# Feed-forward layers: the first two parts of eight heads' weighted sums in one step, the third alone two steps later

## The reference, cut to what matters

```python
x = x + _L0_ffn_ref(_layernorm(x), W_gate, W_qkv)

gating = softmax(x @ W_gate.T); indicator = one_hot(argmax(gating))
q, k, v = split(x @ W_qkv.T, 3)
k_shared = einsum('bth,bthd->btd', indicator, k)
v_shared = einsum('bth,bthd->btd', indicator * max(gating), v)
att = einsum('bhqd,bkd->bhqk', q, k_shared) / sqrt(hd)
att = softmax(where(causal, att, -inf))
y = einsum('bhqk,bkd->bhqd', att, v_shared)
```

## Time and profile before

| | us |
|---|---|
| median of 3 runs | 946.26 |
| lowest, highest | 945.5, 947.89 |
| the profiled execution | 946.92 |
| its span, first to last instruction | 945.2 |
| PE busy | 875.6 (93%) |
| DVE busy | 706.9 (75%) |
| ACT busy | 528.6 (56%) |
| POOL busy | 436.7 (46%) |
| line 1749 (parts 0 and 1), mean of one PE record | 0.38 |

### The profile page before, as it was taken

How to read it: one execution, slowest core, us unless ns; L and a number is a source line. 1 busy time by engine, 2 the same in 40 slices (tenths; PEclk the granted TensorE clock), 3 DMA queues, 4 the chain that set the end, 5 groups by cost and what they waited for, 6 DMA issues and landing times.

```text
span 945.2 us, 19702 instructions
## 1 busy us (share of the span) xinstructions
PE 875.6 (93%) x6510; PEld 684.5 (72%) x6510; DVE 706.9 (75%) x2331; ACT 528.6 (56%) x1378; POOL 436.7 (46%) x682
## 2 busy tenths in 40 slices
PE   5779999889999999987999999999999998999996
PEld 4667777767776777765888788887888776777763
DVE  6678888888778787664868778686868676888873
ACT  6535555454344555436676766757576761555555
POOL 2458888886766556353202121121202022556655
PEclk9789999999999999989999999999999999999999
DMA  6433333223112564102202020202011021132321
GB/s 200 64 55 57 51 51 56 47 44 47 33 32 54 124 125 126 41 14 45 45 2 45 1 45 2 45 1 46 11 35 37 11 34 35 36 65 48 75 48 35
DMA packets 51284, 46.59 MB, mean 49 GB/s; under 512 B 6624, under 2 KB 48624, under 8 KB 51184
## 3 DMA queue, kind: packets, MB, share of 16 engines
q1 hardware_dynamic: 51184, 45.34, 23.8%
HBM read 11.40 MB, written 2.10 MB: 14 GB/s over the span
## 4 chain that ended last, share of the span: by engine, by line
PE 42%; DVE 6%; issue 3%; ACT 2%; POOL 0%; DMA 0%; POOLq 0%; SPq 0%; ACTq 0%; DVEq 0%
PE bank L286 13%; PE bank L1939 6%; PE bank L1889 5%; PE bank L1947 4%; PE bank L1877 4%; PE bank L1711 3%; PE bank L1723 2%; PE bank L1708 2%; DVE weights L1452 1%; PE bank L1749 1%; ACT weights L984 1%; DVE weights L1442 1%; PE bank L1752 1%; DVE arena L1289 1%; PE bank L332 1%
## 5 line engine op out<-in xcount | busy, mean ns | idle before, releaser
L1289 DVE TENSOR_REDUCE arena<-bank 128x2 f32<-128x512 f32 (+1 forms) x192 | 130.6, 683 | 44.7 <-PE bank L1711 44.1
L905 ACT ACTIVATE weights<-bank 128x512 f32<-128x512 f32 x144 | 85.8, 597 | 112.8 <-PE bank L1723 111.8
L984 ACT ACTIVATE weights<-weights,neg_max 128x128 f32<-128x128 f32 (+1 forms) x256 | 113.7, 449 | 32.3 <-DVE neg_max L1442 32.1
L713 POOL TENSOR_SCALAR_AFFINE_SELECT weights<-weights 128x256 f32<-128x256 f32 x144 | 68.0, 473 | 105.9 <-ACT weights L905 105.8
L1711 PE MATMUL bank<-kf_stack,q_stack 96*128 96x128 f32 (+1 forms) x512 | 110.1, 318 | 0.0
L1442 DVE CUSTOM_DVE_ANT_0 weights<-bank,arena 128x128 f32<-128x128 f32 (+1 forms) x256 | 80.6, 352 | 38.3 <-PE bank L1939 36.3
L1939 PE MATMUL bank<-kbT,arena 128*128 128x128 f32 (+1 forms) x512 | 105.1, 328 | 1.0 <-DVE y L421 0.9
L649 POOL TENSOR_SCALAR weights<-weights 128x512 f32<-128x512 f32 x64 | 97.8, 1539 | 12.1 <-ACT weights L808 12.0
L991 ACT ACTIVATE weights<-bank 128x384 f32<-128x384 f32 x128 | 62.7, 490 | 71.2 <-PE bank L1947 70.4
L1452 DVE TENSOR_SCALAR weights<-weights,inv_sum 128x128 f32<-128x128 f32 (+1 forms) x256 | 84.4, 372 | 4.5
L286 PE MATMUL bank<-x_hi,wb_hi 128*128 128x256 f32 x256 | 83.5, 326 | 2.8 <-DVE q_lo L1432 2.8
(11 more groups left out here) (232 smaller groups left out, 2424.9 us busy)
## 6 DMA issues: line engine op xcount, KB each, us to landing
q_stack<-q_hi SPq DMA_DIRECT2D x96, 128.0 KB, 3.8
arena<-arena SPq DMA_DIRECT2D x64, 128.0 KB, 2.5
q_stack<-q_lo SPq DMA_DIRECT2D x48, 128.0 KB, 4.0
ka_stack<-k_hi SPq DMA_DIRECT2D x32, 76.5 KB, 3.8
x_all<-x SPq DMA_DIRECT2D x8, 256.0 KB, 5.4
st_wo<-b_wo SPq DMA_DIRECT2D x8, 256.0 KB, 3.4
arena<-b_wqn SPq DMA_DIRECT2D x8, 256.0 KB, 3.1
out<-x_all SPq DMA_DIRECT2D x8, 256.0 KB, 2.1
```

Of the source, the lines that this page charges most:

```text
L905: a.activation(s["pT"][(STEPS * b + k) % N_PT], p2[k % 2][:, :], ACT.Exp).then_inc(s["exp"], 1)
L984: last = a.activation(p, p, ACT.Exp, scale=-1.0, bias=neg_max[:, h % 4, t:t + 1], accum_out=sums[:, h % 4, t:t + 1])
L1289: v.tensor_reduce(into, p1[k % 2][:, :].rearrange("p (h k) -> p h k", h=n), AX.X, ALU.max, negate=True).then_inc(s["maxed"], 1)
```

## The change

`attend_f` takes a flag in place of the part's number: without it parts 0 and 1 are issued in one go, with it part 2. Octet 1's first parts move from steps 11 and 1 to step 1, its third stays at step 3. Octet 0's move from steps 5 and 7 to step 7, its third stays at step 9. The matmuls are the same in number and form, and their waits (`oT`, `v_sel`, `causal`) move with part 0.

```diff
-                def attend_f(b, o, part):
+                def attend_f(b, o, second):
...
-                    if part == 0:
+                    if not second:
...
-                    pe.wait_ge(*at(s, "causal", b, 6 * o + (6 if part == 2 else 4)))
-                    for j in range(G):
+                    pe.wait_ge(*at(s, "causal", b, 6 * o + (6 if second else 4)))
+                    for part, j in itertools.product((2,) if second else (0, 1), range(G)):
...
-                    if part == 2:
+                    if second:
                         last.then_inc(s["o_ps"], 1)
...
                     if k in (1, 3) and there(b - 2):
-                        attend_f(b - 2, 1, (k + 1) // 2)
-                    if k in (5, 7, 9, 11) and there(b - 1):
-                        attend_f(b - 1, k // 11, (k - 5) // 2 % 3)
+                        attend_f(b - 2, 1, k == 3)
+                    if k in (7, 9) and there(b - 1):
+                        attend_f(b - 1, 0, k == 9)
```

## The result

| | before | after |
|---|---|---|
| median (14 runs each) | 947.01 us | 949.10 us |
| lowest, highest | 944.7, 948.11 | 946.41, 952.25 |
| after / before | | 1.0025, interval 1.0016 to 1.0034 |
| the profiled execution, its span | 946.92, 945.2 | 948.95, 947.2 |
| mean granted clock of the profiled execution | 0.974 | 0.971 |

The change costs 2.1 us where I forecast 1.3 us of gain; 949.1 lies outside the range. PE is busy 3.6 us less and the kernel is still slower. Three executions that took 997 us or more (two of `keep_oct0`, one of the kernel before) are left out of all medians and ratios.

The account below looks back on a forecast made before the run. PE bounds the kernel in the large, but key copies and the DVE decide at the merges; +1.2 + 0.4 - 0.5 - 0.3 - 1.5 - 0.6 = -1.3 us from 946.26 gives 945.0 us, range 942.7 to 948.5.

Parts of the forecast that it names:

- Octet 1, step 11 to step 1: Batch transitions: step 0 gains 0.32 us, step 1 pays 0.43, so 0.11 lost at each of eleven, sum +1.2.
- Start-up 0.05: Step 0 of a batch: PE starts 0.05 us after ACT has written the stacked keys.
- The rival of the late start-up: Step 0: PE starts 0.37 us or more after the keys, each transition loses 0.43; 948.5 to 949.0, chance 0.08 (start-up over 0.3).
- Octet 0, step 5 to step 7: Interior batches: the DVE decides, so PE's 0.33 us buys nothing; only the gate copies gain 0.09 a batch, sum -0.5.
- The copies: Two DVE gate copies after step 5's projection: 0.24 us in place of 0.33, 0.09 off the DVE's chain.
- Batch 6: Both layers, no normalization any more: the gate copy waits 0.98 us for PE, so the earlier projection gives -0.76 twice.
- Other queues ... that it slows the DVE by some hundredths: POOL's masking comes up to 0.76 us sooner beside DVE work; an effect of hundredths a batch, possible in both directions.
- the -0.3: Batch 1 of FFN1: the gate copy waits 0.18 us more for PE, so with the 0.09 octet 0's merge gains 0.3 once.
- The gain of step 0 is lost whole: +0.4: Batch 2 of FFN0: step 0's projection waits 1.07 us for the DVE (x_lo) anyway, so the merge costs +0.4.
- The ends, taken as 0: Four merges from batch 7 to 8 and in batch 8: each from -0.22 to +0.43 us, taken as 0.

Follow-up runs that it names:

- keep_oct0: The changed kernel with octet 0 of the first batch of FFN0 again in steps 5 and 7: 949.12 us, ratio 1.0021 to the kernel before.
- oct1_only: The kernel before with only octet 1 merged at step 1, octet 0 left at steps 5, 7 and 9: 944.66 us, ratio 0.9986.
- the shifted kernels: The kernel before with four or eight dummy matmuls in step 0 of batch 3, FFN0, delaying all later work: 948.89 and 948.59 us.

## Why the prediction was wrong

- **Octet 1, step 11 to step 1: right.** Start-up 0.05, gain 0.30 for 0.32, loss 0.43, together +0.13 a transition for +0.11 (+0.12 by the batch of oct1_only). The rival of the late start-up, which gives 948.5 to 949.0, hits the number by accident: the batch grew by 0.09 and not by 0.34.
- **Octet 0, step 5 to step 7: right, but for 0.05 a batch.** The copies gave their 0.09; line 1316 beside POOL took 0.05 back. The interior of both layers came to +0.55 where I had +0.5 (to +0.8 against the second profile of before, whose FFN0 is 0.25 shorter). Batch 6 gave -0.77 and -0.78 for -0.76.
- **"Other queues ... that it slows the DVE by some hundredths": the first step that failed.** I saw that POOL's work moves up and gave it hundredths in both directions, without laying POOL's timeline beside the DVE's at each batch. In batch 1 of FFN0 a foreign POOL operation of 1.09 us starts just behind the DVE's small operations; moved up, it costs 0.75. I had read only the chain of an interior batch, where POOL has nothing but masks. In FFN1's batch 1 the -0.3 was lost in the same way, and a -0.40 of the clock ahead of it hid that.
- **"The gain of step 0 is lost whole: +0.4" (batch 2 of FFN0): the second.** The term was right (0.37). What was missing is that idle time has a price of its own: taking work out of a stretch in which PE waits anyway leaves it emptier, and behind two such stretches the clock fell to half for 3 us: +1.5. The prediction took the clock as 1.00 and had no term for it.
- **The ends, taken as 0.** They came out at +0.2 and +0.3 off in the profiled pair, but the shifted kernels show that this is no property of the merges: it is where the falls of the clock land.
- **Sum.** Predicted -1.3; with +0.75 for the collision and +1.5 for the clock that makes +0.95, and with the 0.5 by which the ends came out off, +1.45. The profiles give 690.03 - 688.60 = +1.43 from the first turn on. The remaining 0.6 of the profiled pair lies in the first attention, ahead of the change, where two profiles of the kernel before differ by 1.3 among themselves. That the sum closes to 0.02 is partly luck, since the -0.3 of FFN1's batch 1 stands in it and came from the clock. The forecast of 945.0 also started from 946.26, the median of three runs, where fourteen have 947.01.

What stays open: the rule by which a starved stretch gets a fall or doesn't. Two idle stretches in a row brought it in FFN0, neither did without the other; a delay of 0.9 us moved others about. Why the changed kernel is at half clock at its end for 3.5 us in place of 2.2, and the one with both early merges undone at 442 and 933, where the kernel before isn't, was not found.

## What to carry to other kernels

Before taking work out of an engine's list, look whether that engine waits behind it: if it does, the work is free where it is, and for PE the emptier stretch may cost clock on top. The same merge gave +0.12 a batch on the side of the wait and -0.25 on the other side of it (both parts at step 11), so try both places of a pair. When something in another engine's list comes sooner, lay that list beside the DVE's at every batch that is not like the others (the first ones above all, where an earlier layer is still running).

## What I had not expected of the hardware

- A DVE operation of 0.19 us on 128x32 elements took 1.03 us beside a POOL tensor_tensor of 1.09 us and ended 0.05 us behind it, in all six profiles with that merge; with the list shifted by 0.8 us it was not touched. A start of POOL 0.01 us ahead was enough to hold line 1316.
- Behind 1.53 and 1.99 us of idle time, PE worked at half clock for 3 us. Dummy matmuls in the second gap kept it at full clock, without making the projection behind it later.
- Behind the first attention two profiles of one program agree to 0.1 us in nearly every stage, falls of the clock included, while 0.9 us of extra work lengthens one later stage by 1.2 us and shortens another by 1.27.
